# Moving the end of a sort and its ranking among the first steps of the second attention

## The reference, cut to what matters

```python
x = x + _L0_gnn_ref(_layernorm(x), adj, ...)
x = x + _L0_ffn_ref(_layernorm(x), gate_w, gate_b, w1, b1, w2, b2)
x = x + _L1_gnn_ref(_layernorm(x), adj, W, a, bias)
x = x + _L1_ffn_ref(_layernorm(x), W_gat, att_src, att_dst, ..., edge_index)

def _L1_gnn_ref(x, mask, W, a, bias):
    hidden = x W^T;  attn = leaky_relu(attn1[:, :, None] + attn2[:, None, :])
    attn = softmax(where(mask > 0, attn, attn - 1e12))
    return attn @ hidden + bias
# in _L1_ffn_ref, per edge and then per destination node:
e = leaky_relu(a_src[src] + a_dst[dst]);  ee = exp(e - segment_max(e, dst)[dst])
agg = segment_sum(h[src] * ee / (segment_sum(ee, dst)[dst] + 1e-16), dst)
```

## Time and profile before

| What | us |
|---|---|
| median of three runs (3112.32 to 3117.3) | 3113.96 |
| span of the profiled execution | 3601.8 |
| experts and sort, from the first turn to the last scatter | 684.0 to 1243.3 |
| ranking | 1247.2 to 1283.4 |
| second attention, from the first combine to the last search | 1283.5 to 1789.0 |
| loop of the sparse layer | about 1950 to 3520 |

### The profile page before, as it was taken

One profiled execution on the slowest core, in us unless ns is written; L12 is line 12 of the kernel. 1 busy time (PEld: TensorE's weight loads), 2 busy tenths in 40 slices (PEclk: granted clock), 3 DMA queues, 4 the chain that ended last, 5 costly groups with the idle time before them and its releaser, 6 DMA issues. The chain is left out here.

```text
span 3601.8 us, 31245 instructions
## 1 busy us (share of the span) xinstructions
PE 1935.1 (54%) x8829; PEld 1316.8 (37%) x8829; DVE 2257.8 (63%) x4422; ACT 1215.1 (34%) x2447; POOL 1857.5 (52%) x1723
## 2 busy tenths in 40 slices
PE   1776642387878645567432455454544444454555
PEld 1555542255655434456311222232222222222223
DVE  8999886989999965554223454454553444544547
ACT  2676754244444323455311122122212122121222
POOL 5400248554544444445575656655655656656561
PEclk9998865699999867777555676676776677767768
DMA  5792001011111121101111111111111111111111
GB/s 198 250 391 84 16 23 39 24 40 37 46 44 41 36 60 40 56 20 23 42 27 23 32 33 32 32 28 38 32 33 32 32 28 31 38 28 32 37 29 30
DMA packets 170130, 192.35 MB, mean 53 GB/s; under 512 B 59241, under 2 KB 126096, under 8 KB 169008
## 3 DMA queue, kind: packets, MB, share of 16 engines
q1 hardware_dynamic: 107616, 118.69, 9.9%
q0 software_dynamic: 57088, 62.48, 8.4%
q10 hardware_dynamic: 5328, 9.97, 0.7%
HBM read 91.70 MB, written 105.25 MB: 55 GB/s over the span
## 5 line engine op out<-in xcount | busy, mean ns | idle before, releaser
L1518 POOL DMA_INDIRECT edge_rows<-node_table,edge_ids x1024 | 1006.5, 983 | 646.2 <-POOLq L1243 345.9
L1646 PE MATMUL x_b_hid<-x_featT,x_w 128*128 128x512 f32 x512 | 362.3, 854 | 281.4 <-PEq L1243 93.5
L1146 POOL DMA_INDIRECT token_results<-arena,token_of x160 | 251.1, 1569 | 294.3 <-ACT arena L1082 216.9
L583 DVE TENSOR_TENSOR sort_ping<-sort_pong 128x1024 f32<-128x1024 f32 (+1 forms) x232 | 395.1, 1744 | 11.3 <-issue 3.8
L1158 POOL DMA_INDIRECT arena<-keys,row_ids x256 | 249.3, 974 | 288.6 <-DVE counts L821 181.0
L583 DVE TENSOR_TENSOR sort_pong<-sort_ping 128x1024 f32<-128x1024 f32 (+1 forms) x230 | 389.9, 1736 | 8.7 <-ACT sort_ping L1016 3.7
L1139 POOL DMA_INDIRECT slots<-arena,send x128 | 177.8, 1389 | 371.9 <-ACT arena L1038 336.9
L1640 PE MATMUL x_b_featT<-ident,x_feat 128*128 128x128 f32 x128 | 34.8, 428 | 581.0 <-issue 385.3
L1653 PEld LDWEIGHTS x_b_res<-x_w,x_hid 128*128 128x128 f32 x2048 | 276.1, 216 | 152.1 <-issue 152.1
L1653 PE MATMUL x_b_res<-x_w,x_hid 128*128 128x128 f32 x2048 | 303.9, 307 | 39.8 <-issue 39.8
L1646 PEld LDWEIGHTS x_b_hid<-x_featT,x_w 128*128 128x128 f32 x512 | 118.9, 262 | 500.2 <-issue 300.9
(11 more groups left out here) (346 smaller groups left out, 4059.0 us busy)
## 6 DMA issues: line engine op xcount, KB each, us to landing
edge_table<-zeros SPq DMA_DIRECT2D x8, 5120.0 KB, 35.7
edge_rows<-node_table,edge_ids POOLq DMA_INDIRECT x1024
arena<-slots SPq DMA_DIRECT2D x40, 260.0 KB
slots<-zeros SPq DMA_DIRECT2D x2, 5120.0 KB, 24.4
edge_table<-edge_rows SPq DMA_DIRECT2D x64, 160.0 KB
out_dram<-x_y ACTq DMA_DIRECT2D x33, 256.0 KB
x<-in_x_dram SPq DMA_DIRECT2D x4, 2048.0 KB, 20.2
adjacent<-in_adj_dram SPq DMA_DIRECT2D x32, 256.0 KB, 2.7
```

What stands on the lines that cost most here:

```text
L583: step(dve.tensor_tensor(vb[:, :, t, :], va[:, :, 0, :], va[:, :, 1, :], op))
L1146: pool.indirect_dma_start(rows_dram, bass.IndirectOffsetOnAxis(token_of[:, n % 4, r:r + 1], 0), res[:, n % 2, r, :], None, bounds_check=TO ...
L1518: pool.indirect_dma_start(rows[:, u, c, :], None, table_dram, bass.IndirectOffsetOnAxis(ids[:, u, c:c + 1], 0)).then_inc(rows_in[u], 16)
L1646: pe.matmul(b_hid[:, c % 2, :], w1[:, c // HC1, c % HC1 * P:(c % HC1 + 1) * P], featT[:, :], start=True, stop=True).then_inc(hid_mm, 1)
```

## The change

The sort now stops when its seventh crossing is back in the rows. The 12 passes along the rows that are left are taken in steps -3 to 2 of the second attention: two pieces a step up to n = 1, the rest at n = 2 (`SORTED_BY`). The ranking becomes a generator, `rank_keys`, of which one piece runs in each of steps 3 to 7; PE counts two batches behind each of its steps 4 to 7 (`COUNTED_AT`) and sums behind step 7. It uses other PSUM banks. Searches start at n = 9 and run at every step, and at every step of the projection's tail. Groups are combined two at a time in steps -3 and -2 only; the norms of later groups move from steps 1, 9, 17 to 3, 11, 19. SP writes the keys behind its 21st load of results instead of behind its second. Of the passes over the whole table that make the ids, those behind the load of the sources (L850 to L853) move from n = 14 to n = 18; L847 stays at n = 11. In `TURNS_AFTER` the 24 later turns stand one to seven half-steps later. ACT no longer waits for `ranked_s`; PE waits for it at n = 11.

```diff
-        ROOTED_AT, BEHIND_AT = {1: 1, 9: 2, 17: 3}, {1: 1, 9: 2, 17: 3}
+        NORMED_AT = {3: 1, 11: 2, 19: 3}
+        SORTED_BY, COUNTED_AT, SEARCHED_FROM = 2, {4: (0, 1), 5: (2, 3), 6: (4, 5), 7: (6, 7)}, 9
...
-        TURNS_AFTER = {-1: (0, 1, 2, 3), 8: (4,), 9: (5, 6, 7), 18: (8,), 19: (9, 10, 11), 28: (12,), 29: (13,), 30: (14,), 31: (15,),
-                       40: (16,), 41: (17,), 42: (18,), 43: (19,), 52: (20,), 53: (21,), 55: (22,), 56: (23,), 65: (24,), 66: (25,), 68: (26,), 70: (27,)}
+        TURNS_AFTER = {-1: (0, 1, 2, 3), 9: (4,), 10: (5, 6, 7), 20: (8,), 21: (9, 10, 11), 31: (12,), 32: (13,), 33: (14,), 34: (15,),
+                       44: (16,), 45: (17,), 46: (18,), 47: (19,), 58: (20,), 59: (21,), 61: (22,), 62: (23,), 72: (24,), 73: (25,), 75: (26,), 77: (27,)}
...
-            for _ in sorter:
-                pass
+            crossed = 0
+            while crossed < LEVELS:
+                crossed += next(sorter) == "back"
+
+            def rank_keys():
...
+                for c in range(FAN // BATCH):
+                    ge(dve, counted_s, c - 1)
...
+                    if c % 2:
+                        yield
+                dve.wait_ge(counted_s, FAN // BATCH)
+                dve.tensor_copy(held[:, :], b_held).then_inc(rank, 1)
+                dve.wait_ge(summed, 2)
...
+                dve.sem_inc(ranked_s, 1)
+                yield
...
-                for _ in range(2 if joined < 2 * CHUNK else 1):
+                for _ in range(2 if n < -1 else 1):
...
+                if n < SORTED_BY:
+                    advance(2)
+                if n == SORTED_BY:
+                    for _ in sorter:
+                        pass
+                    dve.sem_inc(sorted_s, 1)
+                    ranker = rank_keys()
...
+                if SORTED_BY < n <= SORTED_BY + 1 + len(COUNTED_AT):
+                    next(ranker)
...
-                if n == CHUNK + 6:
+                if n == CHUNK + 10:
...
-                if n >= 0 and n % 4 != 3:
+                if n >= SEARCHED_FROM:
                     search()
...
-                if n % 4 == 3 and searched[0] < SEARCHES // SEARCH:
+                if searched[0] < SEARCHES // SEARCH:
                     search()
...
-                if n == 1:
+                if n == 2 * CHUNK + SORTED_BY + 2:
                     sp.wait_ge(sorted_s, 1)
...
             for n in range(-3, GROUPS + LAG):
                 att1.pe_step(pe, n, n % 4)
+                for batch in COUNTED_AT.get(n, ()):
+                    count_keys(batch)
+                if n == max(COUNTED_AT):
+                    sum_counts()
+                if n == LAG - 1:
+                    pe.wait_ge(ranked_s, 1)
...
-            act.wait_ge(ranked_s, 1)
```

More of the change, by code:

```diff
@@ L522, in front @@
         held_v = held.rearrange("p (q m) -> p q m", m=MATES)
[L523 removed]
+        b_held, b_upto, b_whole = banks[:, 1, 0:2 * P], banks[:, 3, 0:P], banks[:, 1, 2 * P:3 * P]
         span_s, rank, hot, counted_s, summed, ranked_s = (sem(f"rank_{n}") for n in ("span", "step", "hot", "counted", "summed", "done"))
@@ L762, in _ @@
             join()
-            for _ in sorter:
-                pass
-            joined = 0
[L766 to L779, removed]
@@ L780, in _ @@
-            link(dve.tensor_copy(span[:, :], span_i[:, :]))
-            for c in range(FAN // BATCH):
-                ge(dve, counted_s, c - 1)
-                cols = slice(c * BATCH, (c + 1) * BATCH)
-                dve.tensor_tensor(hot_node[:, c % 2, :, :], span[:, 0:P].unsqueeze(1).to_broadcast([P, BATCH, P]),
-                                  part[:, 0, cols].unsqueeze(2).to_broadcast([P, BATCH, P]), ALU.is_equal).then_inc(hot, 1)
-                dve.tensor_tensor(hot_graph[:, c % 2, :, :], span[:, P:3 * P].unsqueeze(1).to_broadcast([P, BATCH, 2 * P]),
-                                  part[:, 1, cols].unsqueeze(2).to_broadcast([P, BATCH, 2 * P]), ALU.is_equal).then_inc(hot, 1)
@@ L788, in _ @@
-            link(dve.memset(att1.right[:, :, :, FEAT:FEAT + 1], 1.0))
-            dve.wait_ge(counted_s, FAN // BATCH)
-            dve.tensor_copy(held[:, :], b_held).then_inc(rank, 1)
-            dve.wait_ge(summed, 2)
-            rows_f = found[:, 1, :]
-            below_0, below_1 = below[:, 0:P], below[:, P:2 * P]
-            link(dve.tensor_copy(whole[:, 0:P], b_whole))
-            link(dve.tensor_tensor_scan(below_0, ones[:, 0:1].to_broadcast([P, P]), whole[:, 0:P], 0.0, ALU.mult, ALU.add))
@@ L805, in _ @@
                 joined += 1
+            link(dve.memset(att1.right[:, :, :, FEAT:FEAT + 1], 1.0))
             dve.wait_ge(got_stats, CHUNK)
@@ L844, in _ @@
                     gat.dve(dve, n - LAG)
+                if n < SORTED_BY:
[5 more added lines that the diff above has]
+                    ranker = rank_keys()
+                    table, tiles = from_to["sorted"]
+                    tiles_u = tiles[:, :].bitcast(U32)
+                if SORTED_BY < n <= SORTED_BY + 1 + len(COUNTED_AT):
+                    next(ranker)
                 if n == CHUNK + 3:
```

64 lines of the change are left out of this document (41 added, 23 removed).

## The result

The changed kernel takes 3235.05 us (median of 4 runs, 3230.82 to 3238.59) against 3115.63 us for the kernel before: a ratio of 1.0383, 95% interval 1.037 to 1.0396, or 119 us more. I had forecast 24 us more, and a range up to 3172.

A forecast was written before the change was run, and what follows sets the result against it. It took attention steps to be bound by a circle of DVE and PE releasing each other, lengthened by moved DVE work: -39 + 65 + 8.6 - 6.9 - 4 = +24, 3114 + 24 = 3138 us, range 3098 to 3172.

The forecast's parts named there:

- The seam: Between experts and second attention: first combine at about 1245 in place of 1283.5, a gain of 39 us.
- The twelve steps: First twelve attention steps, L296 of n = -3 to n = 9: 171 us, counted as +65 over 106 without pauses.
- the circle: Attention steps: DVE and PE release each other in turn; DVE work put behind L296 lengthens the step one for one.
- PE's slower level: First twelve attention steps: summed step by step with PE at its slower clock, they take 174 us.
- The pauses: DVE's "remote" waits ahead of L296 in the first twelve steps, 33.5 us, taken to belong to POOL's gathers and move later.
- the rival: POOL becomes the bound in the searches: 322 us of gathers from about 1432 to 1754, +78, 3192 us; chance 0.14.
- the 488 us: Whole profiled execution of the kernel before: its span of 3601.8 us lay 488 us above the median of 3113.96.
- the chain without pauses: In the POOL rival's sum, the attention's other chain after the change, without pauses, would end at about 1700.
- The ids' wait: Table passes for the ids: the 6.89 us wait for loaded sources goes, -6.9 us.
- the searches' extra work: Steps 9 to 32: a search each, 24 in place of 18, 8.6 us more.
- The tail: End of the attention: eight searches in the first eight of eleven steps, a gain of 4 us, between 8 and 0.
- PE's waits for the sort: Experts' stage: PE waits 22.8 us for the sort's halves; later turns gain 2 us, bounds 0 and 22.8.

The follow-up runs named there:

- disturbed trace: First profiled execution of the unedited kernel before, the one the prediction used: span 3601.8 us, 488 us more than its timed runs.
- the clean one: Second profiled execution of the kernel before, no edit: span 3114.2 us, its one timed run 3116.23 us.
- the first experiment: The kernel before profiled once more, no edit: span 3114.2 us, its one timed run 3116.23 us.
- the eighth experiment: The changed kernel with no searches between the steps of the attention's tail, the last eight following it: 3227.01 us.
- the fifth experiment: The changed kernel with the old table of turns alone: 3234.69 us against 3235.05.
- the third experiment: The changed kernel with the old table of turns and the sort run out ahead of the first combine, ranking and searches left moved: 3184.99 us.

## Why the prediction was wrong

**The seam.** Right: 39 us were forecast, 36.9 measured, with the first combine at 1248.2 (1245 forecast), and the sort's last passes across done at 1226.6 (1230 forecast), where DVE then waited 21.56 us for the first load of results. In the four kernels with the new table the first combine came between 1242.0 and 1249.0, so the 2 us of difference say nothing.

**The twelve steps.** Right in kind, and nearly in size. The moved work lay in the circle and beside nothing: 173.8 us after, where the steps' own sum gave 174 at PE's slower level and the forecast took 171. Step 2, from 1342.17 to 1363.59, took 21.4 us (20.9 forecast). Where the sum went off was before's own stretch, 94.2 us and not 106. The prediction took away the "remote" pauses ahead of L296 alone, and these were not the only ones. The disturbed trace has 12.8 us of waits ahead of L287 in this stretch as well, which the prediction does not take up and of which the clean one shows none:

```profile
DVE arena L287 <- issue: 6.9, 3, 2.8
DVE arena L287 <- ACT arena L181: 5.9, 3, 3.0
```

The growth was thus 80 us and not 65. The busy time by stretch for the clean stretch of before and for after (PE, PEld, DVE, ACT, POOL, PE's clock, DMA share, GB/s):

```profile
1307.90:1402.08 94.18, 64.63 (x398) 54.99 (x398) 77.21 (x225) 57.43 (x136) 65.00 (x68) 0.88 0.25 69
```

```profile
1269.82:1443.60 173.78, 87.52 (x470) 73.17 (x470) 149.52 (x262) 56.03 (x133) 8.29 (x10) 0.74 0.11 35
```

DVE was busy for 77 of 94 us, 82%, and not for 78 of 140, 56%. There was never much idle time to fill. By the Trainium skill (Perfetto Trace Analysis, Optimization Strategy) stages with different busiest engines may gain when they are interleaved; here the stage that took the sort in had the same busiest engine as the sort, and the idle time of the row that seemed to speak for it was not there in a clean execution.

**The pauses.** Right that they would not stay in these steps, wrong in what I tied them to. They belong to one execution, not to POOL's gathers: in the clean stretch of before POOL is busy for 65.0 us with 68 instructions, and no pause follows.

**The step that failed** is the choice between the circle and POOL's queue: the sum has no term for the queue, so POOL's later start was put at nothing. The prediction had the rival, its mechanism and nearly its numbers: first gather at 1432 (1433.3 measured), last at 1754 (1763.8), the point from which it decides (8.4 us a search). It was set aside by one sentence, that the 488 us "have few other places to lie, so the pace without the profiler should be quicker". The pace was 330.5 / 32 = 10.3 us a search, above the point by two microseconds. The trace that was at hand spoke against that sentence: of the 985 waits "issue" between the sparse layer's gathers, 300.3 us in all, the longest is 0.3 us (the row stands in the first experiment). So they are alike, a pace and not a pause, while waits of 181.0 us for DVE's counts and 345.9 us for POOL's sequencer stood in the same rows. In the clean trace these two are 38.5 and 25.1 us; their excess, 463 us, is where nearly all of the 488 us were.

**The second error, of size.** Even the rival's sum of +78 fell short of the measured +119, since I let the chain without pauses end at about 1700 after, which is 1676 for before. The clean trace begins its last search at 1652 and ends its tail at 1630. I had done the sum of POOL's queue for after only; done for before, 1284 + 322 gives 1606 for a queue without waits, against 1754, a difference of 148, and this is an upper bound for what POOL alone can lose that I did not put down. The measured loss is that bound less 34 us that POOL gained by never waiting, and more the 7 us of the tail.

**The circle, taken alone,** came out near the forecast. By the estimate in the eighth experiment, a kernel that POOL did not hold up would have been some 30 us slower than before; 24 were forecast. That closeness is in part luck, since the growth of the stretch was 15 us too small in the sum, and no run shows such a kernel.

**Behind the steps.** The ids' wait is gone, as forecast, but neither this nor the searches' extra work counts: in steps 9 to 32 DVE waits 35 us for keys. The tail, where I had credited 4 us, cost 7: eight searches with about 8 us of waiting each stood ahead of its L389.

**PE's waits for the sort** fell from 23.2 to 17.0 us, 6 where I took 2, and this brought the end nothing in this pair, as the fifth experiment shows.

## What to carry to other kernels

Work that waits for one result is a queue of its own with a length (here 32 searches of 10 us): before the step that produces this result is moved later, add the queue's length to the new start, in the kernel before and in the one after, and compare it with the other chain. What waits for the queue's results should not stand ahead of the other chain's last steps; in the tail of the changed kernel this cost 8 us. A stage that hides work beside another engine's (the sort under the experts) should give that work up only to a stage where the same engine is idle. When a profiled execution is longer than the timed runs, find the excess in the rows whose lengths scatter; rows whose single lengths are all alike show a true pace.

## What the runs showed of the hardware that I had not expected

POOL's indirect scatters last longer while DVE's passes run. Two variants of the changed kernel show it, which differ only in where the sort is run out: the third experiment, with the sort's passes beside the scatters, and the fifth, where DVE has nothing to do there. These are the scatters of the experts' results that start between 1200 and 1247, in this order:

```profile
L1170 POOL DMA_INDIRECT token_results<-arena,token_of x20 | 34.3, 1714 | 21.8 <-ACT arena L1107 16.9 <-issue 4.9
```

```profile
L1170 POOL DMA_INDIRECT token_results<-arena,token_of x20 | 19.5, 973 | 34.2 <-ACT arena L1107 29.3 <-issue 4.9
```

1.71 us each against 0.97. The clean trace of before has 1.72 us. In the changed kernel with its own table, where DVE is busy until 1226.6, the 16 of this stretch took 1.24 us each. The end comes later too, if by less, because POOL also waits less for ACT: from the start of PE's last L994 group to the last scatter it took 12.3 us in the third experiment and 9.9 in the fifth. What in DVE's passes does this was not tried.

And a profiled execution can carry pauses of up to 25 us at waits for other engines, 488 us in all, while single instructions keep their lengths: the search gathers took 974 ns each in the disturbed execution and 978 in the clean one.
